# A two-block transformer kernel: unscaled queries, VectorE row statistics, key chunks first, rotated planes made in the first steps

## The reference

```python
ctrl = hidden @ W_ctrl + b_ctrl        # update gate, angles, candidate, q, k, v, alpha, beta, output gate
q, k, v = (heads(_dwconv_silu(t, w)) for t, w in ...)   # 4 taps over time, then silu; 16 heads of 8
q = q * rsqrt(sum(q * q, -1, keepdims=True) + 1e-12)
k = k * rsqrt(sum(k * k, -1, keepdims=True) + 1e-12)
# each step t, for the vector state and for every head's 8x8 state S:
rot = stack([x1 * ca - x2 * sa, x1 * sa + x2 * ca])     # x1, x2 = 2x2 blocks times the vector state
vec_new = u * rot + (1 - u) * cand
S_new = at * S + bt * (kt[:, None] * (vt - S^T kt)[None, :])
read = S_new^T qt
# after the scan:
m = read * rsqrt(mean(read * read, -1) + 1e-6) * rms_m_w
out = (concat([m, rmsnorm(vec_states)], -1) @ W_out + b_out) * sigmoid(output gate)
```

## Time and profile before

| | us |
|---|---|
| median of 3 runs | 655.72 |
| lowest and highest run | 652.77, 656.79 |
| profiled execution: its time | 655.12 |
| profiled execution: its span | 653.0 |

### The profile page before, as it was taken

One profiled execution on the slowest core, in us unless ns is written; L12 is line 12 of the kernel. 1 busy time (PEld: TensorE's weight loads), 2 busy tenths in 40 slices (PEclk: granted clock), 3 DMA queues, 4 the chain that ended last, 5 costly groups with the idle time before them and its releaser, 6 DMA issues.

```text
span 653.0 us, 14371 instructions
## 1 busy us (share of the span) xinstructions
PE 566.2 (87%) x4639; PEld 479.6 (73%) x4639; DVE 475.1 (73%) x1380; ACT 427.5 (65%) x1032; POOL 383.4 (59%) x434
## 2 busy tenths in 40 slices
PE   0889999999999899989999589876965977798896
PEld 0767999769995899959997357744744755586785
DVE  6655458865688457874312699799999999997946
ACT  1563567746675467645686688978877887786443
POOL 5354045710475025734555323786999999998984
PEclk9989999999999999979999698968979887989999
DMA  8944553136321653125322000000000000000002
GB/s 291 346 149 47 161 120 66 55 58 166 74 65 46 92 147 65 54 55 74 71 53 77 23 1 2 1 2 1 1 0 2 1 1 1 1 2 1 3 2 66
DMA packets 104122, 39.85 MB, mean 61 GB/s; under 512 B 85906, under 2 KB 96178, under 8 KB 103922
## 3 DMA queue, kind: packets, MB, share of 16 engines
q1 hardware_dynamic: 98018, 29.34, 19.9%
q0 software_dynamic: 4480, 9.30, 4.2%
q10 hardware_dynamic: 1552, 0.30, 0.2%
HBM read 20.32 MB, written 18.59 MB: 60 GB/s over the span
## 4 chain that ended last, share of the span: by engine, by line
PE 51%; POOL 21%; DVE 18%; ACT 4%; issue 3%; DMA 2%; ACTq 1%; POOLq 0%; DVEq 0%; SPq 0%
PE PS L2332 17%; PE PS L2317 16%; POOL W1s L864 9%; DVE W2s L1403 4%; POOL wT L784 4%; PE PS L2270 2%; PE PS L2233 2%; POOL two_planes L786 2%; POOL slotbuf L788 2%; DMA oscale<-in_L_attn_out_scale_dram 2%; PE PS L2260 1%; ACT W1s L1948 1%; POOL hbuf L790 1%; POOL two_planes L789 1%; PE PS L2670 1%
## 5 line engine op out<-in xcount | busy, mean ns | idle before, releaser
L748 POOL DMA_INDIRECT sorted_x<-xrow,pos x93 | 90.9, 977 | 134.6 <-DVE pos L1216 107.8
L2332 PE MATMUL PS<-W2s,hbuf 128*128 x992 | 139.3, 284 | 0.0
L2317 PE MATMUL PS<-hbuf,swt 128*128 128x128 f32 x992 | 131.7, 276 | 1.0 <-DVE hbuf L1281 0.9
L2332 PEld LDWEIGHTS PS<-W2s,hbuf 128*128 128x128 f32 x992 | 126.7, 191 | 0.5
L2317 PEld LDWEIGHTS PS<-hbuf,swt 128*128 128x128 f32 x992 | 120.9, 192 | 1.6 <-issue 0.9
L1733 ACT ACTIVATE hbuf<-PS 128x512 f32<-128x512 f32 x124 | 73.2, 590 | 45.6 <-PE PS L2317 44.4
L1741 ACT ACTIVATE xrow<-PS,tags 128x144 f32<-128x144 f32 (+1 forms) x124 | 46.9, 378 | 41.8 <-PE PS L2332 39.6
L1948 ACT ACTIVATE W1s<-W1s,ab 128x128 f32<-128x128 f32 x168 | 51.3, 393 | 15.4 <-DVE W1s L1551 15.3
L2509 PE MATMUL PS<-ewT,xT 128*128 128x512 f32 x64 | 38.6, 734 | 21.0 <-ACT W2s L1999 21.0
L864 POOL TENSOR_TENSOR W1s<-W1s,kT 128x1024 f32<-128x1024 f32 x22 | 52.4, 2388 | 7.0 <-DVE W1s L1551 5.8
L753 POOL DMA_INDIRECT results<-xrow,pos x31 | 31.2, 1007 | 37.1 <-ACT xrow L1741 25.1
(11 more groups left out here) (419 smaller groups left out, 1324.4 us busy)
## 6 DMA issues: line engine op xcount, KB each, us to landing
hbuf<-sorted_x SPq DMA_DIRECT2D x224, 32.0 KB
sorted_x<-slotbuf SPq DMA_DIRECT2D x9, 520.0 KB, 2.9
W1s<-in_L_ffn_W_dram SPq DMA_DIRECT2D x1, 4096.0 KB, 20.6
sorted_x<-slotbuf SPq DMA_DIRECT2D x1, 2015.0 KB, 11.2
sorted_x<-xrow,pos POOLq DMA_INDIRECT x109, 2.4
sorted_x<-slotbuf SPq DMA_DIRECT2D x3, 455.0 KB, 2.8
xres<-in_L_attn_x_dram SPq DMA_DIRECT2D x4, 256.0 KB, 4.1
xrow<-results SPq DMA_DIRECT2D x4, 256.0 KB, 4.1
```

Of the source, the lines that this page charges most:

```text
L748: pool.indirect_dma_start(xs_dram[l + 1][:, :], bass.IndirectOffsetOnAxis(ap=pos[:, t:t + 1], axis=0), xrow[:, t % NR, 0:XW], None).then_i ...
L2317: m = pe.matmul(PS[:, 2 + n, f * P:(f + 1) * P], w1st[:, (c - 1) % WB, f * P:(f + 1) * P], xring[:, (c - 1) % R, :], start=True, stop=True)
L2332: m = pe.matmul(PS[:, 4 + n, 0:w], hTs[:, n, f * P:(f + 1) * P], W2s[:, f * YW:f * YW + (E - 1) * NF + w][:, bass.ds(w2, w)], start=(f == ...
```

## The change

- *Queries keep their length.* Their squares per chunk, their length, root and reciprocal go, and with them POOL's product over all queries. A read then is too long by the query's length |q|. The RMS norm of the read takes this out if its small constant is scaled too: `1e-6 * |q|^2 + 1e-18` stands in its place. POOL squares the queries in step 1, PE sums them by head before step 3's reads, ACT scales the sums in step 4, and `mean_squares` adds them by one more matmul with the identity. Its four matmuls of 128 repeated columns become four of 16.
- *Row statistics.* For the first two of four groups DVE's `row_stats` (the function of the first layer norm) takes the place of sum and squares.
- *Angles.* The last two of the five reducing steps go from DVE to POOL, where they are three instructions.
- *Keys first.* PE turns all four key groups before the values' inputs. `chunks` works on 64x64 corners of the identity: one transpose and one matmul per step in place of two matmuls over 128 rows. `alpha_beta` is spread over four places.
- *ACT.* Sine and cosine follow the last value input, then a table load, the keys' root, a table load, and the gates' tanh. Queries are copied around the last silu.
- *Rotated planes.* `turn_plane`, `cos_part` and the sine's products move into steps 0 to 3; the update and keep planes start one step later (4 instead of 3).

```diff
-    JOBS = (("angles0", 7), ("angles1", 0), ("k0", 1), ("k1", 7), ("k2", 0), ("k3", 1), ("q0", 7), ("v0", 1), ("q1", 0), ("q2", 6),
-            ("q3", 1), ("cand00", 4), ("cand01", 5), ("v1", 6), ("cand10", 4), ("cand11", 5), ("v2", 6), ("u00", 4), ("u01", 5),
-            ("v3", 6), ("u10", 4), ("u11", 5))
+    JOBS = (("angles0", 7), ("angles1", 0), ("k0", 1), ("k1", 7), ("k2", 0), ("k3", 1), ("q0", 7), ("q1", 0), ("q2", 6), ("q3", 1),
+            ("v0", 5), ("cand00", 4), ("cand01", 5), ("v1", 6), ("cand10", 4), ("cand11", 5), ("v2", 6), ("v3", 6), ("u00", 4),
+            ("u01", 5), ("u10", 4), ("u11", 5))
...
+            pool.wait_ge(ang_red, 1)
+            step(pool.tensor_scalar(cosp, kp, -TWO_PI_LO, None, ALU.mult))
+            step(pool.tensor_tensor(angp, angp, cosp, ALU.add))
+            pool.tensor_scalar(angp, angp, PI_DOWN, -PI_DOWN, ALU.min, ALU.max).then_inc(ang_red, 1)
+            squared_lengths()
...
-            squared_lengths(1)
-            plane_summed(0)
-            pool.wait_ge(unit_ready, 2)
-            q_all = Qc.rearrange("p t h i -> p (t h) i")
-            step(pool.tensor_tensor(q_all, q_all, nstd[:, 1, :].unsqueeze(2).to_broadcast([P, C * HP, HD]), ALU.mult))
...
                 if t < VEC_AT:
-                    if t == 2:
+                    if t == 0:
+                        pool.wait_ge(sincos, 2)
+                        pool.tensor_tensor(cosp, cosp, cosp, ALU.mult).then_inc(cos_ready, 1)
+                    elif t == 1:
+                        pool.wait_ge(post_ready, 2 * B)
+                        for b in range(B):
+                            half = slice(b * S, (b + 1) * S)
+                            o = pool.tensor_tensor(query_squares[:, half], post[1][:, half], post[1][:, half], ALU.mult)
+                        o.then_inc(sq_ready, 1)
+                    elif t == 3:
+                        plane_summed(0)
                         plane_summed(1)
...
+                if g < BY_STATS:
+                    return row_stats(g)
...
-            row_squares(0)
-            row_squares(1)
             norm_roots(0)
+            norm_roots(1)
             row_squares(2)
-            norm_roots(1)
+            norm_roots(2)
             tokens_T(1, 0)
             row_squares(3)
-            norm_roots(2)
             tokens_T(1, 1)
...
             for t in range(C):
...
+                if t in (0, 2, 3):
+                    rotation((t + 1) // 2)
+                if t in (1, 4):
+                    plane(zpl[:, t // 4, :], ACT.Silu, pbias[:, 2 + t // 4:3 + t // 4])
...
+                if t == QUERY_EPS_AT:
+                    act.wait_ge(pd_mm, 6)
+                    act.activation(query_eps, PS[:, 1, 0:NT * H], ACT.Identity, scale=1e-6, bias=eps_q[:, 0:1]).then_inc(len_ready, 1)
...
-                if 3 <= t < 7:
-                    (update_plane if t % 2 else keep_plane)((t - 3) // 2)
+                if 4 <= t < 8:
+                    (keep_plane if t % 2 else update_plane)((t - 4) // 2)
...
                         v = by_step(post[n], g * SB + t)
-                        for q in range(HS):
-                            m = pe.matmul(o[part_rows(q), t * DP:(t + 1) * DP], v, ident[:, part_rows(q)], start=True, stop=True)
+                        a, z = part_rows(0), part_rows(1)
+                        pe.transpose(o[a, t * DP:(t + 1) * DP], v[a], ident[a, a])
+                        m = pe.matmul(o[z, t * DP:(t + 1) * DP], v[z], ident[z, z], start=True, stop=True)
...
-            alpha_beta(range(0, 10))
+            alpha_beta(range(0, 8))
             conv_input(1, 2)
             conv_input(1, 3)
-            chunks(0, (0, 1))
+            alpha_beta(range(8, 14))
+            chunks(0, range(NG))
             conv_input(2, 0)
             conv_input(2, 1)
-            chunks(0, (2,))
+            alpha_beta(range(14, 20))
             conv_input(2, 2)
             conv_input(2, 3)
-            chunks(0, (3,))
-            alpha_beta(range(10, C))
-            chunks(1, (0,))
+            alpha_beta(range(20, C))
+            chunks(1, range(NG))
             chunks(2, (0,))
-            chunks(1, range(1, NG))
...
+                if t == QUERY_EPS_AT - 1:
+                    pe.wait_ge(sq_ready, NG + 1)
+                    pe.wait_ge(sh1, 1)
+                    for n in range(NT):
+                        m = pe.matmul(PS[:, 1, n * H:(n + 1) * H], query_squares[:, n * P:(n + 1) * P], headsel[:, :], start=True, stop=True)
+                    m.then_inc(pd_mm, 1)
...
+                pe.matmul(PS[:, half, 0:G * H], ident[:, :], query_eps[:, half * G * H:(half + 1) * G * H], start=True, stop=False)
                 for t in range(G):
                     tt = half * G + t
-                    r = P // H
-                    m = pe.matmul(PS[:, half, t * H:(t + r) * H].rearrange("p (r h) -> p r h", r=r),
-                                  osq[:, tt * P:(tt + 1) * P], headmean[:, :].unsqueeze(1).to_broadcast([P, r, H]),
-                                  start=True, stop=True)
+                    m = pe.matmul(PS[:, half, t * H:(t + 1) * H], osq[:, tt * P:(tt + 1) * P], headmean[:, :], start=False, stop=(t == G - 1))
```

More of the change, by code:

```diff
@@ L1904, in _ @@
             silu(0)
[L1905 removed]
             conv_input(1, 2)
             conv_input(1, 3)
[L1908 to L1915 removed]
+            silu(1)
+            for g in range(NG):
+                chunked(0, Kc, g)
             conv_input(2, 0)
@@ L1954, in _, with rotation @@
             decayed(0)
-            for g in range(1, NG):
-                chunked(1, Qc, g)
+            def rotation(n):
+                if n == 0:
+                    act.wait_ge(sincos, 2)
+                    for i in range(2):
+                        act.activation(mpl[:, 0, i, :], sinp, ACT.Copy, scale=nwblk[:, 2 * i + 1:2 * i + 2]).then_inc(sincos, 1)
+                    return
+                for m in ((1, 3), (0, 2))[n - 1]:
+                    w = slice(m, m + 1)
+                    act.wait_ge(cos_ready, 1 if n == 1 else 3 + m // 2)
+                    act.activation(cos_part[m], cosp, ACT.Identity, bias=wblk[:, w], scale=n2wblk[:, w]).then_inc(cos_ready, 1)
             def plane_banks():
@@ L2054, in roots @@
                 act.wait_ge(oms_mm, n + 1)
[L2055 to L2056 removed]
+                act.activation(ostd[:, half * G * H:(half + 1) * G * H], PS[:, half, 0:G * H], ACT.Sqrt).then_inc(ostd_ready, 1)
             def spread(n):
```

196 lines of the change are left out of this document (99 added, 97 removed).

## The result

| | before | changed |
|---|---|---|
| median, us | 654.76 (4 runs) | 693.70 (4 runs) |
| lowest and highest | 652.77, 656.79 | 688.57, 704.80 |
| profiled execution: time, span | 655.12, 653.0 | 692.52, 690.8 |
| mean granted clock | 0.945 | 0.900 |

The ratio is 1.057, with a 95% interval of 1.049 to 1.064. The changed kernel is 39 us slower, where 651.1 was forecast. The page of the changed kernel says where to look: the chain that ends last, and the clock row.

A forecast was written before the change was run, and what follows sets the result against it. No engine bounds the whole program; its end hangs on when DVE finishes step 4, which releases POOL's unbroken work. Step 4 ends 4.4 us early: 655.1 - 4.4 + 0.2 (update plane) + 0.2 (tail) = 651.1 us, range 647.0 to 655.0.

The forecast's parts named there:

- the key chunks: PE's key groups before the values: 24 records, 1.6 us a group instead of 2.1; convolution 5 begins 2.4 us earlier.
- Rival D: Key groups: alternating transposes and matmuls empty PE at each change, 4.7 us a group, +15.5, 666.6 us; chance 0.06.
- The number of groups: Chunk groups on the path: each microsecond a group costs four before step 0, one through the value group, five in all.
- A's price: Key groups: the new chunks save nothing, a group stays at 2.1 us, +2.6, 653.7 us; chance 0.14.
- C's mechanism: Key groups: two halves of the array work together, a group near 1.3 us or less, 649.5 to 648.4 us; chance 0.15.
- Rival E: Ahead of step 0: ACT's queue gives back layer norm's gain, step 0 begins as before, 654.5 us; chance 0.06.
- the stretch before step 0: Convolution 5 to step 0: ACT is the later one; DVE's first state write at 411.95 instead of 415.30, -3.35 us.
- Layer norm: DVE's statistics for two groups let the first convolution begin 2.8 us earlier and the second 2.3 us earlier.
- Steps 0 to 4: DVE's early steps: -1.6 wait, -1.75 reciprocal, -0.7 key product, +2.7 turned planes; choosing the experts stays at 4.0.
- rival B: Early steps: ACT or POOL holds them, turned planes blocked by POOL or update plane late, 2.4 us, 653.5 us; chance 0.13.
- After step 4: ACT makes the update plane one step later, still about in time for POOL; 0.2 us charged.
- Tail: End of program: a mean square of 8 records becomes 10 smaller ones, +0.2 us at most for the two that count.

The follow-up runs named there:

- e1: Changed kernel with the chunks' old form back (two matmuls over 128 rows per step): 660.23 us median, ratio 1.001.
- e3: Changed kernel with the chunks' transpose made a plain matmul, so two plain matmuls on opposite 64x64 corners: 655.24 us (one run).
- e13: e3 with DVE's row statistics for the first two layer norm groups undone: 657.76 us, ratio 1.003.
- e8: e7 without POOL's two sums of the cosine's part of the planes, so its result lacks them: ratio 1.004.
- e4: Changed kernel with a group's eight transposes first, then its eight matmuls: 667.30 us median, ratio 1.013.
- e14: e3 again, unchanged, with more runs: 656.74 us, ratio 1.004.
- e12: e3 with mean squares 128 columns wide again and the queries' length not added, so not a full version: 654.91 us, ratio 0.997.
- e7: e3 with four filling identity matmuls behind each of the last two groups of mean squares: ratio 1.002.
- e11: e3 with filling identity matmuls where PE waits, four ahead of the third group of mean squares and two behind the fourth: 656.47 us, ratio 1.001.
- e9: e7 with the first of POOL's two sums of a turned plane moved from step 3 to step 2: ratio 1.004.
- e2: Kernel before with only the chunks' new form (alternating transpose and matmul on 64x64 corners): 689.66 us (one run).
- e10: Kernel before with only the chunks turned by plain matmuls on 64x64 corners: ratio 0.996.

## Why the prediction was wrong

**The step that failed is the key chunks.** I priced the group by a record rate, 24 x 0.065 = 1.6 us. It takes 4.5 at the full clock and 5.24 at the lower, more than the upper bound I had set (4.7, every instruction waiting for the one before; that bound counted a plain matmul of two records as one of 0.292 us). Rival D named the mechanism, that transposes and matmuls which alternate don't overlap, and its price for a group was nearly right. It had a chance of 0.06 on the strength of one sentence, that the trace shows such a change once per step with no gap visible. That was weak evidence: a timeline whose ends are modelled can't show a gap of 0.16 us behind a row of eight. The record rate I used in its place came from instructions of one kind only.

**The number of groups failed as well.** I counted five groups on the path, four of keys and one of values, which made D 666.6. At 5.24 us PE bounds everything from convolution 4 to step 5 (the chain lies on it from 382.48 to 482.31), and all twelve groups stand on the path: 12 x (5.24 - 1.98) = 39.1 us by e1's and the changed kernel's groups; the sums in the table differ by 37.7, or 40.4 without the last part. Nine of the twelve stand ahead of the first state write, 29.3 us by the same sum, and A to B is 29.7 longer. "Each us a group costs five in all" was true only while PE was not the bound. The lower clock is part of this: 5.24 us for a group where eight steps of 0.56 are 4.5, so about 0.76 a group, some 9 us of the 39 by my estimate; and the router's 32 records take 7.00 us, 3.74 before. No run holds the clock up under the alternating form, so the clock's share was not measured.

**Rivals A and C**, priced by records too, fell with it. The transposes of a 64x64 corner did take one record each (96 for 96), so A's price, drawn from the rule of the Trainium skill (TensorEngine Tiling (Array Packing), "Restrictions") that column tiling disables the transpose mode for FP32, didn't come. The rule itself is neither borne out nor refuted: the trace doesn't show in which division of the array the transposes ran. C's mechanism, two parts of the array at work together, is real, but seen only between matmuls of one kind: e3's group is 1.76 us. Rival E, that step 0 begins as before, is not what e3 shows either (below).

**Rest of the forecast, seen in e3.** With cheap chunks the forecast of the stretch before step 0 holds in its order: convolution 5 at 393.95 behind a wait of 1.99 us (394.3 and 2.4 forecast), the first state write at 411.64, let go by ACT (411.95 forecast), turned planes of 1.28 us each, no wait for ACT in step 1, a key product of 0.42. Counted from the last attention sum the gain is 2.6 us, not 3.35, as that sum came 1.1 us earlier in e3's run.

- *Layer norm*: the size is right (2.2 us; 2.3 to 2.8 forecast), the reason wrong. e13 has it without the statistics; the order of ACT's roots and DVE's scaling is the likely cause.
- *Steps 0 to 4*: forecast -1.05 after the first state write, measured +0.9. The term that failed is "choosing the experts in step 4 stays at 4.0": it grew by 2.94 us through POOL's plane sums. I had the mechanism, and looked for it at the wrong instructions (rival B: the turned planes, which ran freely). The Trainium skill (SBUF — State Buffer, "Who interferes with whom") has VectorE and GpSimd hold a port pair as an exclusive lock; e3 and e8 agree (2.09 and 2.07 us beside the sums, 0.28 and 0.29 without them).
- *After step 4*: "I charge 0.2" holds only while step 4 is late. As soon as B to C is 3.5 us shorter (e8), the update plane, late on PE and ACT, takes nearly all of it.
- *Tail*: +0.2 forecast. At the full clock it is +0.2 (changed kernel and e4, 8.77 and 8.78 for 8.54). In e1, e3, e13 and e14 the granted clock fell there and it is +2.9. It stayed up in e12 (wide mean squares) and in e7, e8 and e11 (filling), but fell in e9, whose filling is e7's. So the fallen clock is 2.7 of the 2.9 us; what decides whether it falls was not settled.

So the rest of the change was worth 1.6 us in e12's trace (its sum against before's), where 4.0 was forecast: the first state write gave 2.7 and not 3.35, steps 0 to 4 cost 0.9 and not -1.05, and the end cost 0.2 and not 0.4.

## What to carry to other kernels

Don't price an instruction mix by a rate that was measured on one kind of instruction: transposes and plain matmuls that alternated one by one on opposite corners of the array cost PE 0.16 us at each change here, more than one of their records (0.12 us at the same clock). Make both plain: two plain matmuls on opposite corners ran together (1.76 us a group). All of one kind first took most of the loss away, but at 2.5 to 3.0 us a group it stayed behind the old form's 1.98. And when a term is multiplied by the number of times it stands on the path, ask at what size of the term that number changes: here 5 became 12.

## What the runs showed of the hardware that was not expected

- A plain matmul of the identity on a 64x64 corner is faster than the transpose of the same corner beside a matmul: 0.22 us against 0.56 a step, though it is one record more.
- The granted clock went to 0.50 while the profile showed PE busy for 5.00 of 5.00 us. So a PE shown as busy throughout did not mean that the clock was kept.
- In the last 15 us, mean squares of 16 columns in place of 128 were followed by a fall of the clock in four of the six profiled runs without filling (e1, e3, e13, e14), not in the changed kernel's or e4's, whose instructions there are the same, and in one of the four with filling (e9). The clock was kept in all four runs with the wider form (before, e2, e10, e12).
